# Experts with hand-overs two pairs apart instead of one, final addition first in its step, shared expert padded to 128 rows, copy of the turned inner rows on VectorE

## What is computed

```python
x = x + attention(layernorm(x))          # 16 query heads, 4 key heads of width 16, rope, causal
h = layernorm(x)
topv, topi = top_k(h @ gate_w.T, 8)      # 64 experts
W = softmax(topv) placed at topi
gu = einsum('nh,eih->nei', h, gu_w)      # 64 gate and 64 up columns for each expert
inter_w = silu(gate) * up * W[:, :, None]
out = einsum('nei,ehi->nh', inter_w, dp_w)
sh_out = (silu(h @ sh_gate_w.T) * (h @ sh_up_w.T)) @ sh_down_w.T
out = out + sigmoid(h @ sh_gate1_w.T) * sh_out
x = x + out
```

## Time and profile before

| | us |
|---|---|
| median of 3 runs | 1461.35 |
| lowest and highest | 1455.36, 1462.63 |
| the profiled execution, whole time | 1475.3 |
| its span, first to last instruction | 1473.5 |
| mean granted TensorE clock | 0.892 |

### The profile page before, as it was taken

The page is one execution under the profiler, slowest core; times in us unless marked ns, Lnnn a source line. Parts: engine busy times, 40 slices in busy tenths (PEclk is TensorE's granted clock), DMA queues, the critical chain, the costliest instruction groups (busy, mean ns, idle before and its releaser), DMA issues. The chain is left out here.

```text
span 1473.5 us, 26911 instructions
## 1 busy us (share of the span) xinstructions
PE 1155.0 (78%) x7746; PEld 865.3 (59%) x7746; DVE 710.1 (48%) x2210; ACT 665.7 (45%) x1650; POOL 729.7 (50%) x978
## 2 busy tenths in 40 slices
PE   3799989898998989988874048788788888878871
PEld 2566666565665666665543047677677677667650
DVE  2566766566564665655422411111244444444455
ACT  2466555555554455543321024444444445444530
POOL 3101127556374463744556735555555555556541
PEclk9799999999898999988866569999899999999985
DMA  2687757212122121211229655555567777666534
GB/s 77 203 274 239 244 176 249 75 52 91 40 97 71 52 83 47 94 61 64 72 76 325 206 158 157 159 156 160 207 228 259 263 241 261 222 238 219 173 113 153
DMA packets 144735, 233.45 MB, mean 158 GB/s; under 512 B 19831, under 2 KB 122438, under 8 KB 139216
## 3 DMA queue, kind: packets, MB, share of 16 engines
q1 hardware_dynamic: 69776, 101.07, 21.6%
q0 software_dynamic: 27648, 69.28, 13.1%
q10 hardware_dynamic: 47168, 61.35, 12.9%
HBM read 107.32 MB, written 132.66 MB: 163 GB/s over the span
## 5 line engine op out<-in xcount | busy, mean ns | idle before, releaser
L1299 POOL DMA_INDIRECT res_d<-y,dst_i x320 | 319.8, 999 | 261.0 <-ACT y L1151 141.5
L817 DVE TENSOR_REDUCE nmax<-ps 128x1 f32<-128x512 f32 (+3 forms) x448 | 226.2, 532 | 183.2 <-PE ps L474 150.3
L424 POOL DMA_INDIRECT rows_d<-pay,slot_i x256 | 257.4, 1005 | 74.4 <-issue 70.7
L684 ACT ACTIVATE wgu_s<-ps 128x512 f32<-128x512 f32 x320 | 192.0, 601 | 198.9 <-PE ps L515 168.7
L1239 PE MATMUL psB<-wgu_s,xT 128*128 x1280 | 184.0, 290 | 34.2 <-issue 22.7
L472 PE MATMUL ps<-kT,qT 96*128 96x512 f32 (+3 forms) x512 | 198.3, 432 | 9.1 <-DVE nmax L817 6.8
L513 PE MATMUL ps<-qT,kT 128*128 128x512 f32 (+3 forms) x512 | 194.5, 424 | 3.4 <-ACT qT L697 3.2
L1239 PEld LDWEIGHTS psB<-wgu_s,xT 128*128 128x128 f32 x1280 | 166.2, 203 | 43.2 <-issue 42.7
L1066 DVE TENSOR_TENSOR inner<-inner,psB 128x128 f32<-128x128 f32 x160 | 45.6, 285 | 288.4 <-ACT inner L1138 228.4
L1257 PE MATMUL psD<-wdp_s,innerT 128*128 x640 | 178.2, 404 | 0.0
L1131 ACT COPY xT<-psA 128x512 f32<-128x512 f32 x160 | 95.2, 595 | 118.2 <-PE psA L1228 92.0
(11 more groups left out here) (194 smaller groups left out, 1696.5 us busy)
## 6 DMA issues: line engine op xcount, KB each, us to landing
rows_d<-blank ACTq DMA_DIRECT2D x8, 5440.0 KB, 18.9
xg<-rows_d SPq DMA_DIRECT2D x320, 136.0 KB
yk<-res_d SPq DMA_DIRECT2D x32, 1024.0 KB
wgu_s<-wgu_in ACTq DMA_DIRECT2D x8, 1024.0 KB
x_d<-x SPq DMA_DIRECT2D x32, 192.5 KB
xs<-x_d SPq DMA_DIRECT2D x32, 192.5 KB
res_d<-y,dst_i POOLq DMA_INDIRECT x320
wgu_s<-x_in SPq DMA_DIRECT2D x32, 128.0 KB, 2.7
```

The source lines that it names most:

```text
L424: pool.indirect_dma_start(rows_d, bass.IndirectOffsetOnAxis(ap=slot_i[par][:, t, k:k + 1], axis=0), pay[par][:, t, :], None).then_inc(s_sc ...
L684: act.activation(pexp[p % 4][:, s, :], ps2[:, (5 * p + s) % 2, :], ACT.Exp, scale=HEAD_D ** -0.5).then_inc(s_exp, 1)
L817: return dve.tensor_reduce(nmax[u][:, tile, heads[0]:heads[-1] + 1], src, AX.X, ALU.max, negate=True)
L1299: pool.indirect_dma_start(res_d, bass.IndirectOffsetOnAxis(ap=dst_i[:, j % G:j % G + 1], axis=0), y[:, j % Y, :], None, bounds_check=ROUTE ...
```

## The change

- The distances in the chain become GATE = 2, TURN = 4, DOWN = 6 steps (1, 2, 3 before), and the order on TensorE in a step is turned round: down(i-6), shared, turn_inner(i-4), gate_up(i-2), turn_x(i). ScalarE does y_copy(i-6), shT_copy, silu(i-2), xT_copy(i).
- xT, inner and innerT get A = 3 buffers. STEPS is 160 + 7. The sums of a tile, the loads of a tile and its turns move along: LOADED_BEFORE 26, SUMMED_AFTER 12.
- innerT_copy goes from ScalarE to VectorE (tensor_copy out of PSUM) and stands before gated.
- psC gets a second bank, psS goes: the shared expert uses columns 2P to 4P of the psC bank that turn_inner of its step uses. sh and shT are padded with zeros to 128 columns and rows.
- mix comes after all eight additions, writes fin itself, and is the first operation of VectorE in step 5 of the tile. The eight additions take steps 0 to 3, turn_shared comes in step 2 and down_shared in step 4.
- One DMA loads the rows of a pair (256 rows) instead of one for each block; y has 10 slots instead of 12, dst_i 32 instead of 16.
- Tiles of the batch before the last begin every third step instead of every second. late_sums are then tiles 27 to 31.

```diff
-            G, R, Y = 16, 4, 12
+            G, R, Y, A = 16, 4, 10, 3
+            GATE, TURN, DOWN = 2, 4, 6
-            dst_i = sb("dst_i", [P, G], I32)
+            dst_i = sb("dst_i", [P, 2 * G], I32)
-            psC = ps("psC", [P, SEQ])
-            psS = ps("psS", [P, SEQ])
+            psC = ps("psC", [P, 2, SEQ])
-            STEPS = PAIRS + 4
-            LOADED_BEFORE, SUMMED_AFTER, SUM_STEPS = 20, 9, 4
+            STEPS = PAIRS + DOWN + 1
+            LOADED_BEFORE, SUMMED_AFTER = 26, 12
+            SUM_STEPS, TURN_SHARED, DOWN_SHARED, MIX = 4, 2, 4, 5
 ...
-                return 4 if tile // TILES == BATCH - 2 else 8
+                return 6 if tile // TILES == BATCH - 2 else 8
 ... SyncE
-                for j in range(BLOCKS):
+                for i in range(PAIRS):
+                    j = 2 * i
                     if j >= G:
-                        sp.wait_ge(e_a_ps, (j - G) // 2 + 1)
+                        sp.wait_ge(e_a_ps, i - G // 2 + 1)
                         sp.wait_ge(e_pick, (j - G) // R + 1)
-                    sp.dma_start(xg[:, j % G, :], rows_v[j]).then_inc(e_x[j % G], 16)
-                    while tile < ALL_TILES and load_turn(tile) <= j:
+                    sp.dma_start(xg[:, j % G:j % G + 2, :], rows_v[i]).then_inc(e_x[i % (G // 2)], 16)
+                    while tile < ALL_TILES and load_turn(tile) <= j + 1:
 ... VectorE
+                def innerT_copy(i):
+                    dve.wait_ge(e_c_ps, i + 1)
+                    if i >= A:
+                        dve.wait_ge(e_d_ps, i - A + 1)
+                    dve.tensor_copy(innerT[:, i % A].rearrange("p b n -> p (b n)"), psC[:, i % 2, 0:2 * P]).then_inc(e_c, 1)
                 def mix(tile):
                     u = tile % 2
-                    dve.wait_ge(c_acc[u], TOP * (tile // 2) + TOP - 1)
+                    dve.wait_ge(c_acc[u], TOP * (tile // 2 + 1))
                     dve.wait_ge(c_y_ps, tile + 1)
-                    dve.tensor_tensor(acc[:, u], psS[:, P:P + D], acc[:, u], ALU.add).then_inc(c_mix, 1)
+                    step = STEPS if tile in late_sums else sum_step(tile) + DOWN_SHARED
+                    dve.wait_ge(e_c, min(PAIRS, step - TURN + 1))
+                    if tile >= 2:
+                        dve.wait_ge(c_out[u], 16 * (tile // 2))
+                    dve.tensor_tensor(fin[:, u], psC[:, shared_bank[tile], 2 * P:2 * P + D], acc[:, u],
+                                      ALU.add).then_inc(c_mix, 1)
                 for i in range(STEPS):
-                    if 0 <= i - 1 < PAIRS:
-                        gated(i - 1)
+                    for tile, s in tile_at(i):
+                        if s == MIX:
+                            mix(tile)
+                    if 0 <= i - TURN < PAIRS:
+                        innerT_copy(i - TURN)
+                    if 0 <= i - GATE < PAIRS:
+                        gated(i - GATE)
 ... ScalarE
                 for i in range(STEPS):
+                    if 0 <= i - DOWN < PAIRS:
+                        y_copy(i - DOWN)
+                    for tile, s in tile_at(i):
+                        if s == TURN_SHARED:
+                            act.wait_ge(e_c, min(PAIRS, i - TURN + 1))
+                            shT_copy(tile)
+                    if 0 <= i - GATE < PAIRS:
+                        silu(i - GATE)
                     if i < PAIRS:
                         xT_copy(i)
-                    if 0 <= i - 1 < PAIRS:
-                        silu(i - 1)
-                    if 0 <= i - 2 < PAIRS:
-                        innerT_copy(i - 2)
-                    if 0 <= i - 3 < PAIRS:
-                        y_copy(i - 3)
 ... TensorE
                 for i in range(STEPS):
                     if i % 2 == 0 and i < PAIRS:
                         load_offsets(2 * i)
+                    if 0 <= i - DOWN < PAIRS:
+                        down(i - DOWN)
+                    for tile, s in tile_at(i):
+                        if s == DOWN_SHARED:
+                            pe.wait_ge(c_t, tile + 1)
+                    for tile, s in tile_at(i - 1):
+                        if s == MIX:
+                            pe.wait_ge(c_mix, tile + 1)
+                    for tile, s in tile_at(i):
+                        if s == TURN_SHARED:
+                            turn_shared(tile)
+                        if s == DOWN_SHARED:
+                            down_shared(tile)
+                    if 0 <= i - TURN < PAIRS:
+                        turn_inner(i - TURN)
+                    if 0 <= i - GATE < PAIRS:
+                        gate_up(i - GATE)
                     if i < PAIRS:
                         turn_x(i)
-                    if 0 <= i - 1 < PAIRS:
-                        gate_up(i - 1)
-                    if 0 <= i - 2 < PAIRS:
-                        turn_inner(i - 2)
-                    if 0 <= i - 3 < PAIRS:
-                        down(i - 3)
```

More of the change, by code:

```diff
@@ L991, in sum_step @@
                 return (complete(tile) + every(tile) * (tile % TILES)) // 2 + SUMMED_AFTER
-            late_sums = [tile for tile in range(ALL_TILES) if sum_step(tile) + SUM_STEPS >= STEPS]
+            late_sums = [tile for tile in range(ALL_TILES) if sum_step(tile) + MIX >= STEPS]
             def tile_at(step):
                 return [(tile, step - sum_step(tile)) for tile in range(ALL_TILES)
-                        if tile not in late_sums and 0 <= step - sum_step(tile) < SUM_STEPS]
+                        if tile not in late_sums and 0 <= step - sum_step(tile) <= MIX]
+            shared_bank = [(sum_step(tile) if tile not in late_sums else tile) % 2 for tile in range(ALL_TILES)]
             block = ctx.enter_context(nc.Block())
@@ L1079, in add @@
                 def add(tile, k):
-                    u, last = tile % 2, k == TOP - 1
+                    u = tile % 2
                     if k == 0:
@@ L1165, in shT_copy @@
                         act.wait_ge(c_y_ps, tile - 1)
-                    act.copy(shT[:, u], psS[0:INNER, 0:P]).then_inc(c_t, 1)
+                    act.copy(shT[:, u], psC[:, shared_bank[tile], 2 * P:3 * P]).then_inc(c_t, 1)
                 def store(tile):
-                    act.wait_ge(c_acc[tile % 2], TOP * (tile // 2 + 1))
+                    act.wait_ge(c_mix, tile + 1)
                     act.dma_start(out_v[tile], fin[:, tile % 2, :]).then_inc(c_out[tile % 2], 16)
@@ L1184, in _ @@
                             shared(tile)
-                        if s == 1:
-                            shT_copy(tile)
-                    while stored not in late_sums and sum_step(stored) + SUM_STEPS <= i:
+                    while stored not in late_sums and sum_step(stored) + MIX < i:
                         store(stored)
@@ L1238, in gate_up @@
                         for c in range(KC):
-                            last = pe.matmul(psB[:, i % 2, b * GU:(b + 1) * GU], xT[:, i % 2, b, c, :],
+                            last = pe.matmul(psB[:, i % 2, b * GU:(b + 1) * GU], xT[:, i % A, b, c, :],
                                              wgu_s[:, bass.ds(off + c * GU, GU)], start=(c == 0), stop=(c == KC - 1))
@@ L1262, in turn_shared @@
                     pe.wait_ge(c_sh, tile + 1)
-                    if tile >= 1:
-                        pe.wait_ge(c_mix, tile)
-                    pe.transpose(psS[0:INNER, 0:P], sh[:, tile % 2, :], ident).then_inc(c_t_ps, 1)
+                    pe.transpose(psC[:, shared_bank[tile], 2 * P:3 * P], sh[:, tile % 2, :], ident).then_inc(c_t_ps, 1)
                 def down_shared(tile):
                     pe.wait_ge(c_t, tile + 1)
-                    pe.matmul(psS[:, P:P + D], shT[:, tile % 2, :], shd_w[0:INNER, :], start=True, stop=True).then_inc(c_y_ps, 1)
+                    pe.matmul(psC[:, shared_bank[tile], 2 * P:2 * P + D], shT[:, tile % 2, :], shd_w[:],
+                              start=True, stop=True).then_inc(c_y_ps, 1)
                 for i in range(STEPS):
```

91 lines of the change are left out of this document (35 added, 56 removed).

## The result

| | before | changed |
|---|---|---|
| median of the runs (lowest to highest), us | 1461.99 (1455.36 to 1462.92) | 1441.86 (1440.66 to 1442.82) |
| ratio, 95% interval | | 0.9868 (0.9841 to 0.9895) |
| profiled execution, us (its span) | 1475.3 (1473.5) | 1440.66 (1438.9) |

The change takes 20 us off, half of the 41 forecast.

What follows compares the result with a forecast made beforehand. It took GpSimd's scatters, waiting for y because TensorE's results reach ScalarE late while scatters run, as the bound. Its terms, 41 + 5 - 3 - 2 = 41 us off, gave 1461 - 41 = 1420 us median, range 1375 to 1470.

Steps and rivals of the forecast that it cites:

- Part 1: Expert stage: hand-overs two pairs apart make GpSimd's waits for y fewer, 13 to 21 at 2.43 us, 41 us saved.
- No TensorE stop before psB between tiles: Sign that the forecast is right: TensorE's stops of 1 to 1.7 us per cycle are covered by the longer distance.
- Part 4: Final addition after all eight, padded shared expert: up to 3 us more TensorE load, waits unbooked; 0, bounds -5 to +8 us.
- Part 2: Copy of turned inner rows moved to VectorE: 0.42 us each, VectorE about 203 us in 1060 to 1400; cost 0 to 20, taken 0.
- Part 3: Destinations in 32 slots, made six steps before their scatter: GpSimd's waits for them go, 5 us saved, between 0 and 6.
- Parts 5 to 7: Merged row loads 0 (-3 to +3 us); y in 10 slots 0; fill 3 us later, drain 2 us (0 to 5).
- C: Rival: no change, results go through the same slow path whatever the distance, three pairs to a wait; 1461 us, chance 0.14.
- B: Rival: half the gain, since the 100 pairs with tiles gain nothing under the DMA load of the sums; 1445 us, chance 0.14.
- D: Rival: slower, in-order VectorE waits for turned rows and silu, holding up TensorE's down and tile sums; 1481 to 1501, chance 0.12.
- E: Rival: the copy on VectorE stops GpSimd, costing 48 us against the 41; 1468 us, chance 0.04.
- A: Rival: no result is awaited any more and GpSimd becomes the bound; 1332 us, chance 0.11 for anything below 1400.

Runs made afterwards that it cites:

- after2: The changed kernel run again, unaltered, on a chip where results are late: 1440.36 us beside 1462.96 for the kernel before, ratio 0.9839.
- noscat_a: The changed kernel with GpSimd clearing one column instead of each scatter, sums reading other rows: 1298.03 us beside 1462.96 for the kernel before.
- actcopy: The changed kernel with innerT_copy back on ScalarE behind the y copy, where results are on time: 1291.45 us, ratio 0.9934 to the kernel before.
- after3: The changed kernel run again, unaltered, on a chip where results are on time: 1284.94 us beside 1296.94 for the kernel before, ratio 0.9903.
- every6: The kernel before with only the sums of the batch before the last 6 blocks apart, not 4; six runs, first 1285.98 us beside 1296.29.

## Why the prediction was half right

**What bounds the kernel: right, and shown.** Late results, only while scatters run, were the reading of the trace; on the chip of after2, noscat_a takes them away with the scatters, 142 us in all. That it needs such a chip, and is not the kernel's alone, was not in the prediction and could not be seen in one trace.

**Part 1, the distance: the term that was mis-sized.** It said: the third result gets through on time, so a late one comes in four or five pairs and not in three, 13 to 21 fewer rests at 2.43 us, 41 us. The step from there to four or five pairs is the one it called most doubtful. The mechanism is there: runs of two or three pairs have become runs of three or four, and there are 14 to 17 fewer rests. Three things in the term were mis-sized. First, the count: before there was a rest of over 1 us in 160 / 67 = 2.4 pairs, since some stand under the destinations and under issue, and the change brought 3.2 and 3.0 (after2), not four or five. Second, the length: the sum held a rest at 2.43 us. But how late a result is grows while scatters run, whatever the distance, so a longer run is followed by a longer rest: in the 40 pairs without tiles 2.95 and 2.72 us for 2.44, over the whole stage 2.69 and 2.62. All rests together fell by 29 and 24.5 us, where parts 1 and 3 had 46. Third, even that fall is not the distance's alone. The last 19 pairs, where the spacing acts, have 7 to 11 us of it, and the execution of before was a long one, 13 us over its median.

Where neither sums nor spacing act, in the 40 pairs without tiles, the change brought 3.4 us; the forecast's rate would be 41 x 40 / 160 = 10. A pair takes 3.35 us from the first to the last y copy, for 3.54 before and 3.2 to 3.3 forecast. In the 100 pairs with tiles the traces show 14 to 18 us, part of which is the long execution of before. Which of the parts brings these was not separated on a chip where results are late.

**What TensorE waits for: half wrong.** "No TensorE stop before psB between tiles" did not come: its waits there in the expert stage are still 16.4 us in 11 for xT, for 11.1 in 12 before. Under issue they fell from 22.7 to 5.6. Of after:

```profile
PE psB L1245 <- ACT xT L1146: 16.4, 11, 2.5
PE psC L1268 <- DVE fin L1110: 13.5, 12, 5.2
PE psC L1268 <- ACT xT L1146: 12.4, 3, 4.7
PE psC L1253 <- DVE inner L1071: 12.2, 8, 3.0
```

The rows at L1268 are the shared expert's transpose, with the wait for the final addition (c_mix) ahead of it. That wait now stands in front of the pair's own matmuls of its step. In the expert stage the listed waits ahead of turn_inner fell from 44.7 us to 23.5, those ahead of the shared transpose rose from 14.9 to 37.3. Part 4 left these waits unbooked; they took up about as much as the pairs' hand-overs gave back.

**Part 2, the copy: right.** 0.420 us for 0.42, 201 us for 203, and nothing on the path where results are on time (actcopy). Where they are late VectorE waits 43.6 us in 17 times for psC with gated behind; whether that costs time was not tested.

**Part 3, destinations: right in kind, small in size.** Nine waits with 23.6 us under the destinations have become three with 4.1. The forecast took 5 us, since y was late by nearly as much; that is why the row of y alone hardly moves. It is the same pool of rests as part 1, and must not be counted a second time.

**What was not in the sum: the spacing.** The diff changes `every` from 4 to 6, and I named only its cost, tile 27 behind the loop, 2 us. Its gain, 9 to 13 us of 1296 alone, is as large as half of all that was measured. On the chip where results are late no run had it alone, but the last 19 pairs gain the same 9 to 10 us there. If it is worth as much there, which is an estimate from these two rows, some 10 us are left for all the other parts together, against the 46 of parts 1 and 3.

**Parts 5 to 7.** Merged row loads did no harm that shows: SyncE waits longer for the sums (136.4 us in 19 waits for the 99.7 in 13 of the earlier trace rows), yet TensorE waits for no rows. The first y copy comes 1.5 us later after the first turn_x, not 3 (9.7 for 8.2 us); where results are on time it is 2 to 3 us (10.8 in after3, 7.6 to 9.2 in the six of every6). The end did not get longer, 34.5 for 36.4 us.

**Rivals.** C (the lateness is paced by the scatters whatever the distance) is nearly what the stretch without tiles shows in time, 3.4 us of 134.9, though not in its count: there are 11 rests for 14, each longer. B's 1445 was the number closest to 1442, but for another reason than its own, since its pairs without tiles gained least. D's mechanism, TensorE's down behind VectorE's copy, exists and costs 20.5 us of waits at distance one; at distance two it is nearly gone (2.6 us in 4 waits). E did not come: scatters beside the copy take 996 ns for 999. On the other chips it is 1008 in after3, but 1005 in actcopy too, where ScalarE copies. A's condition, no late results, holds on six chips, and GpSimd is the bound there as A has it: 1285 us, but there the kernel before takes 1296 as well.

## What to carry to other kernels

Before a saving is taken from a stop, look at whether the stop is the engine's own or a result that something else holds back; more distance covers a fixed delay, and where the delay grows as long as another engine is busy it makes rests fewer and longer. Rests of one engine that stand under different releasers are one pool: count them all from the time line before and after, number and length, and price each constant in a diff by itself, since here one number gave as much as half of the change. Price also where the last work can lie while the end waits for a transfer.

## What the runs showed of the hardware

- **Results of TensorE can be held back for as long as scatters run.** In the profile after, a psB result reached ScalarE 7.28 us after its modelled end. On the chip of after2 a silu came up to 7.1 us late; without scatters on that chip (noscat_a) it was 0.04 us in the pairs shown and 0.4 at most. The Trainium skill, Perfetto Trace Analysis, section "Tensor Engine Instruction (MATMUL, LD_WEIGHTS)", has the semaphore update follow once PSUM has acknowledged the write. The runs show that what lies between the modelled end and the next engine's start is not a constant.
- **Chips differ by more than most edits.** The kernel before took 1462 us where the result was measured and in the series of after2, and 1296 to 1298 us on six other chips. Whether that is the chip or its condition at the time was not tested. Scatters take 1.0 us on either kind; what differs is the results beside them. Of the 150.5 us between the two profiled spans of the changed kernel (1438.8 in after2, 1288.3 in after3) 124 lie between the first and the last y copy (535.3, 411.6) and 32 before the stage (it starts at 859.3 and 827.6). The ratio of the change was 0.984 to 0.987 on the one and 0.990 on the other.
- **A chip without late results is bound by TensorE and GpSimd almost at once**: 2.41 us a pair by TensorE without tiles, 2.58 by back-to-back scatters, 2.6 to 2.7 measured with tiles at distance two or in the old order.
- **A stop of TensorE can cost its clock.** During the stop of 2.92 us in the profile after, behind one of 0.81, the granted clock fell from 1.00 to 0.50. It stayed there for 6 us, and psB took 1.92 us for 1.06.
